# Moving a square root ahead of other copies, sharing a gated add between three engines, and taking the next norm in two halves, in a one-expert layer of a transformer kernel

## What is computed

```python
x = x + _L0_xcond_ref(_layernorm(x), ctx_1024, ...)
x = x + _L0_ffn_ref(_layernorm(x), ...)
x = x + _L1_xcond_ref(_layernorm(x), ctx_1024, ...)
x = x + _L1_ffn_ref(_layernorm(x), Wg, We, be)       # the one-expert layer
x = x + _L2_xcond_ref(ctx_1024, _layernorm(x), ...)  # window attention
x = x + _L2_ffn_ref(...)
...
def _L1_ffn_ref(x, Wg, We, be):                      # h: x as rows of tokens
    probs = softmax(h @ Wg); best = argmax(probs); gate = max(probs)
    mask = one_hot(best) where the token's place in its expert's queue < cap
    out  = (gate * mask) * (h @ We + be)             # all experts share We, be
def _L2_xcond_ref(encoder_outputs, decoder_h_t, src_len, p_t, W_a, W_c):
    score = decoder_h_t @ W_a @ encoder_outputs.T, masked to a window
    context = (softmax(score) * gauss) @ encoder_outputs
    return tanh(concat(context, decoder_h_t) @ W_c.T)
```

## Time and profile before

| | us |
|---|---|
| median of three runs | 1104.2 |
| lowest, highest | 1101.93, 1104.84 |
| the profiled execution's own time | 1099.49 |
| its span, first to last instruction | 1097.7 |

### The profile page before, as it was taken

The page is one execution under the profiler, slowest core; times in us unless marked ns, Lnnn a source line. Parts: engine busy times, 40 slices in busy tenths (PEclk is TensorE's granted clock), DMA queues, the critical chain, the costliest instruction groups (busy, mean ns, idle before and its releaser), DMA issues. The chain is left out here.

```text
span 1097.7 us, 32356 instructions
## 1 busy us (share of the span) xinstructions
PE 938.4 (85%) x12720; PEld 709.1 (65%) x12720; DVE 754.9 (69%) x1651; ACT 596.6 (54%) x1231; POOL 377.3 (34%) x415
## 2 busy tenths in 40 slices
PE   4689998988889998999976689999978999976993
PEld 2457775455666764677754566679835777755992
DVE  4678786646888857888857676657487888761443
ACT  2656565653556654666646675246654676612561
POOL 5033320425333211333200003846723326064442
PEclk8899999989999999999999799999989999967996
DMA  8499980000000000000020001123310112111225
GB/s 248 134 334 322 290 208 3 1 7 5 2 2 3 3 2 1 2 2 3 3 92 1 1 3 57 45 62 91 99 34 17 35 32 68 50 37 54 71 72 170
DMA packets 82013, 73.12 MB, mean 67 GB/s; under 512 B 7600, under 2 KB 77168, under 8 KB 81872
## 3 DMA queue, kind: packets, MB, share of 16 engines
q1 hardware_dynamic: 76656, 61.49, 20.2%
q0 software_dynamic: 4544, 9.36, 2.5%
q10 hardware_dynamic: 672, 0.27, 0.1%
HBM read 24.42 MB, written 46.46 MB: 65 GB/s over the span
## 5 line engine op out<-in xcount | busy, mean ns | idle before, releaser
L1591 ACT ACTIVATE P_t<-ps_pt 128x512 f32<-128x512 f32 x256 | 146.0, 596 | 137.3 <-PE ps_pt L1914 132.3
L1928 PE MATMUL psT<-VB,P_t 128*64 128x18 f32 x4096 | 165.9, 214 | 26.9 <-ACT P_t L1591 19.9
L1928 PEld LDWEIGHTS psT<-VB,P_t 128*64 128x64 f32 x4096 | 140.4, 137 | 66.0 <-ACT P_t L1591 48.6
L956 DVE TENSOR_REDUCE mx<-ps_sc 128x16 f32<-128x1024 f32 x128 | 150.1, 1215 | 16.7 <-PE ps_sc L1902 16.6
L1914 PE MATMUL ps_pt<-cst,work 128*128 128x128 f32 x1024 | 151.5, 281 | 0.0
L967 DVE TENSOR_TENSOR work<-ps_sc,mx 128x1024 f32<-128x1024 f32 x128 | 150.2, 1215 | 0.0
L1554 ACT ACTIVATE work<-work 128x1024 f32<-128x1024 f32 x128 | 128.2, 1048 | 34.3 <-DVE work L967 34.0
L1914 PEld LDWEIGHTS ps_pt<-cst,work 128*128 128x128 f32 x1024 | 112.2, 142 | 5.5 <-ACT work L1554 1.5
L640 POOL TENSOR_TENSOR kbh<-KT,cst 128x512 f32<-128x512 f32 x64 | 65.2, 1039 | 140.2 <-PE ps_sc L1902 107.0
L640 POOL TENSOR_TENSOR rt<-KT,cst 128x512 f32<-128x512 f32 x64 | 65.5, 1044 | 117.5 <-PE ps_sc L1902 117.4
L763 POOL DMA_INDIRECT ys_dram<-work,to_row x78 | 76.4, 979 | 73.0 <-DVE to_row L1446 38.5
(11 more groups left out here) (333 smaller groups left out, 1658.4 us busy)
## 6 DMA issues: line engine op xcount, KB each, us to landing
xs_dram<-slots SPq DMA_DIRECT2D x1, 17160.0 KB, 57.7
xs_dram<-slots SPq DMA_DIRECT2D x1, 17028.0 KB, 123.0
QT<-ys_dram SPq DMA_DIRECT2D x8, 512.0 KB, 6.1
work<-xs_dram SPq DMA_DIRECT2D x39, 65.0 KB, 1.9
work<-xs_dram SPq DMA_DIRECT2D x39, 64.5 KB, 1.9
VB<-L_ffn_W1b_in SPq DMA_DIRECT2D x8, 258.0 KB, 2.6
ctxT<-ctxT_in SPq DMA_DIRECT2D x4, 512.0 KB, 6.9
X<-x_in SPq DMA_DIRECT2D x4, 512.0 KB, 8.0
```

Source lines behind the costliest of these rows:

```text
L956: v.tensor_reduce(mx4[:, :, HPR * t:HPR * t + HPR], sc[:, :, HPR * t:HPR * t + HPR], AX.X, ALU.max).then_inc(max_ready, 1)
L1591: act.activation(P_t[:, 512 * c:512 * c + 512], ps_pt[:, 512 * (c % 2):512 * (c % 2) + 512], ACT.Copy).then_inc(p_evac, 1)
L1928: mm = pe.matmul(psT[64 * b:64 * b + 64, 144 * t + 18 * g:144 * t + 18 * g + 18], P_t[:, at:at + 64], VB[:, UNIT * u + 2 * t + b, g, :, :] ...
```

## The change

- ACT's Sqrt table is loaded explicitly in the last turns of the third attention, and again after the Exp of the logits.
- `rstds` only takes the root; the wait for the finished norm moves into `normalise`, ahead of the first tile. The root of norm 3 stands ahead of `take_a`; two pieces are taken before the normalised tiles, two after the second chunk.
- The four `take_z` ahead of the gates are gone: after the gates ACT gates the four tiles of each even chunk and takes two mixed pieces after each.
- Pool adds the gated even chunks to `X`; DVE adds the odd chunks in one instruction for each tile that multiplies by the gate and adds (`add_gated`).
- Norm 4 is taken in two halves of 16 tiles. The first half's variance comes behind 16 tiles' statistics, the second half's whole chain behind DVE's first normalised half chunk. `NORM_AT` renumbers the counts of the norms for that.
- TensorE waits for all mixed pieces only at step 1 of `attention2`.

```diff
+        NORM_AT = [0, 1, 2, 3, 4, 6, 7]
...
+            def mixture1():
+                pool.wait_ge(x_updated, TILES * 3)
+                for c in range(0, CHUNKS, 2):
+                    xc = X[:, c * TPC:c * TPC + TPC, :]
+                    pool.wait_ge(y_gated, TPC * (c // 2 + 1))
+                    pool.tensor_tensor(xc, Yt[:, c * CHUNK:c * CHUNK + CHUNK].rearrange("p (t d) -> p t d", d=D), xc,
+                                       ALU.add).then_inc(y_added, 1)
+
...
-            def norms_of(ts, i):
+            def norms_of(ln, ts, i):
                 nonlocal n_ln
-                n = n_ln
-                v.wait_ge(stats_ready, TILES * 6 + ts.stop)
+                n, at = n_ln, NORM_AT[ln] + i
+                v.wait_ge(stats_ready, TILES * ln + ts.stop)
                 variance(ts, ln_step, n)
                 n_ln = n + CHAIN_STEPS
                 def finish():
-                    v.wait_ge(rsqrt_ready, 7 + i)
-                    inverse_root(ts, ln_step, n + 5, root_inverted, 7 + i, norm_ready, 2 * (6 + i) + 1)
+                    v.wait_ge(rsqrt_ready, at + 1)
+                    inverse_root(ts, ln_step, n + 5, root_inverted, at + 1, norm_ready, 2 * at + 1)
...
+            def second_norms(ln):
+                norms_of(ln, slice(TILES // 2, TILES), 1)()
+                v.wait_ge(norm_ready, 2 * NORM_AT[ln] + 4)
...
-                def update(k, turn, u, live):
-                    if live(0):
-                        v.wait_ge(y_gated, TPC * (k + 1))
-                        xc = X[:, bass.ds(k * TPC, TPC), :].rearrange("p t d -> p (t d)")
-                        v.tensor_tensor(xc, Yt[:, bass.ds(k * CHUNK, CHUNK)], xc, ALU.add).then_inc(x_updated, TPC)
-                    if live(1):
-                        for t in range(TPC):
-                            tile_stats(4, (k - 1) * TPC + t)
-
-                pipeline(v, CHUNKS, 2, 1, update)
+                def add_gated(t):
+                    ins = v.scalar_tensor_tensor(X[:, t, :], Yt[:, t * D:t * D + D], gate[:, 1, t:t + 1], X[:, t, :], ALU.mult, ALU.add)
+                    if t % TPC == TPC - 1:
+                        ins.then_inc(x_updated, 2 * TPC)
+
+                pairs = CHUNKS // 2
+                for i in range(pairs + 1):
+                    if i < pairs:
+                        for t in range((2 * i + 1) * TPC, (2 * i + 2) * TPC - 1):
+                            add_gated(t)
+                    if i > 0:
+                        for t in range(8 * i - 8, 8 * i):
+                            tile_stats(4, t)
+                    if i == 2:
+                        finish_first = norms_of(4, slice(0, TILES // 2), 0)
+                    if i < pairs:
+                        v.wait_ge(y_added, i + 1)
+                        add_gated((2 * i + 2) * TPC - 1)
+                    if i == pairs - 1:
+                        finish_first()
...
-                norms(4)
...
                         normalise_half(4, k, u)
+                        if isinstance(k, int) and k == 0:
+                            second_norms(4)
...
             def rstds(ln):
-                act.wait_ge(ln_step, 2 + CHAIN_STEPS * ln + 5)
+                act.wait_ge(ln_step, 2 + CHAIN_STEPS * NORM_AT[ln] + 5)
                 act.activation(lnw[:, 4, :], lnw[:, 3, :], ACT.Sqrt).then_inc(rsqrt_ready, 1)
-                act.wait_ge(norm_ready, 2 * ln + 2)
-
-            def root_of(ts, i):
-                act.wait_ge(ln_step, 2 + CHAIN_STEPS * (6 + i) + 5)
+
+            def root_of(ln, ts, i):
+                act.wait_ge(ln_step, 2 + CHAIN_STEPS * (NORM_AT[ln] + i) + 5)
                 act.activation(lnw[:, 4, ts], lnw[:, 3, ts], ACT.Sqrt).then_inc(rsqrt_ready, 1)
             def normalise(ln, k, u):
-                if ln == 6 and isinstance(k, int) and k == 1:
-                    act.wait_ge(norm_ready, 2 * 7 + 2)
+                if isinstance(k, int) and (k == 0 or k == 1 and ln in (4, 6)):
+                    act.wait_ge(norm_ready, 2 * (NORM_AT[ln] + k) + 2)
...
+                    if l == 2 and u == UNITS:
+                        act.preload_act_table_set("sqrt_and_others")
...
             def mixture1():
-                for c in range(4):
+                rstds(3)
+                for c in range(2):
                     take_a(c)
-                rstds(3)
                 def step(k, turn, u, live):
                     normalise(3, k, u)
+                    if isinstance(k, int) and k == 1:
+                        for c in (2, 3):
+                            take_a(c)
                 pipeline(act, CHUNKS, 2, 0, step)
                 for c in (4, 5):
                     take_a(c)
                 act.wait_ge(route_step, 2)
                 act.activation(e_logit, rt[:, 0, :, :], ACT.Exp).then_inc(route_act, 1)
+                act.preload_act_table_set("sqrt_and_others")
                 for c in (6, 7):
                     take_a(c)
-                for c in range(4):
-                    take_z(c)
                 act.wait_ge(keep_step, 5)
                 act.wait_ge(y_kept, 2 * CHUNKS)
-
-                for k in range(CHUNKS):
+                for k in range(0, CHUNKS, 2):
                     for t in range(k * TPC, k * TPC + TPC):
                         row = Yt[:, t * D:t * D + D]
                         act.activation(row, row, ACT.Copy, scale=gate[:, 1, t:t + 1]).then_inc(y_gated, 1)
-                    if k < 4:
-                        take_z(4 + k)
+                    take_z(k)
+                    take_z(k + 1)
+                root_of(4, slice(0, TILES // 2), 0)
...
-                rstds(4)
...
                         normalise(4, k, u)
+                        if isinstance(k, int) and k == 0:
+                            root_of(4, slice(TILES // 2, TILES), 1)
...
-                pe.wait_ge(z_ready, CHUNKS)
                 def step(k, turn, u, live):
                     s, r = u, (u + 1) % 2
+                    if isinstance(k, int) and k == 1:
+                        pe.wait_ge(z_ready, CHUNKS)
```

More of the change, by code:

```diff
@@ L345, in build @@
         y_gated = sem("y_gated")
+        y_added = sem("y_added")
         a_in_psum = sem("a_in_psum")
@@ L746, in _ @@
             pool.memset(maskR[0:2, :], -4.0 * BIG).then_inc(win_filled, 1)
+            def mixture1():
[5 more added lines that the diff above has]
+                                       ALU.add).then_inc(y_added, 1)
+            mixture1()
             def mixture(m):
@@ L859, in norms @@
                 variance(slice(0, TILES), ln_step, n)
-                v.wait_ge(rsqrt_ready, l + 1)
-                inverse_root(slice(0, TILES), ln_step, n + 5, root_inverted, l + 1, norm_ready, 2 * l + 1)
+                at = NORM_AT[l]
+                v.wait_ge(rsqrt_ready, at + 1)
+                inverse_root(slice(0, TILES), ln_step, n + 5, root_inverted, at + 1, norm_ready, 2 * at + 1)
                 n_ln = n + CHAIN_STEPS
+            def second_norms(ln):
+                norms_of(ln, slice(TILES // 2, TILES), 1)()
+                v.wait_ge(norm_ready, 2 * NORM_AT[ln] + 4)
             def variance(ts, counter, n):
@@ L942, in prepare @@
                 v.wait_ge(w_loaded, W_DMAS * 16)
-                v.wait_ge(norm_ready, 2 * ln + 2)
+                v.wait_ge(norm_ready, 2 * NORM_AT[ln] + 2)
                 pipeline(v, CHUNKS, 2, 2, step)
@@ L1112, in rows @@
                                         ALU.mult, ALU.add).then_inc(xn_half, 1)
-                v.wait_ge(norm_ready, 2 * 5 + 2)
+                v.wait_ge(norm_ready, 2 * NORM_AT[5] + 2)
                 rows(0)
@@ L1363, in step @@
                         v.tensor_tensor(p, p, den[s][:, 1, :].unsqueeze(2).broadcast_to([128, TPC, 128]), ALU.mult).then_inc(p2_ready, 1)
-                v.wait_ge(norm_ready, 2 * 4 + 2)
+                v.wait_ge(norm_ready, 2 * NORM_AT[4] + 2)
                 pipeline(v, CHUNKS, 2, 5, step)
@@ L1471, in mixture @@
                         if q == 1:
-                            finish_first = norms_of(slice(0, TILES // 2), 0)
+                            finish_first = norms_of(6, slice(0, TILES // 2), 0)
                         if q == 2:
                             finish_first()
-            def second_norms():
-                norms_of(slice(TILES // 2, TILES), 1)()
-                v.wait_ge(norm_ready, 2 * 7 + 2)
             attention2()
             mixture(0)
-            prepare(3, 6, tau_s, second_norms)
+            prepare(3, 6, tau_s, lambda: second_norms(6))
             attention(3)
@@ L1746, in mixture @@
                     rstds(ln)
+                    act.wait_ge(norm_ready, 2 * NORM_AT[ln] + 2)
                     act.preload_act_table_set("silu_and_others")
@@ L1802, in _ @@
                 if c == 5:
-                    root_of(slice(0, TILES // 2), 0)
-            act.wait_ge(norm_ready, 2 * 6 + 2)
-            prepare(6, lambda: root_of(slice(TILES // 2, TILES), 1))
+                    root_of(6, slice(0, TILES // 2), 0)
```

(1 more changed line is left out.)

## The result

| | before | after |
|---|---|---|
| median, us | 1103.41 (4 runs, 1101.93 to 1104.84) | 1092.76 (4 runs, 1089.06 to 1093.58) |
| the profiled execution's own time | 1099.49 | 1092.79 |
| its span | 1097.7 | 1091.0 |

The account below looks back on a forecast made before the run. It took waits around ACT's blocked roots and gating, at the router norm and from gates to next norm, as the bound; 5.1 + 5.2 + 0.4 = 10.7 us gave 1093.5, forecast 1091.4 to 1096.3, widened 2.7 either side.

Parts of the forecast that it names:

- A: First place, norm before the router: root ahead of context pieces brings the first kept router output 5.1 us earlier.
- B: Second place, gates (G) to the first transposed chunk's copy: G+18.1 instead of 23.27 us, a gain of 5.2.
- C: Third attention: ACT's first key copy no longer waits for the complete norm, a gain of 0.4 us.
- D: TensorE's clock at the second place: same course as before, 3.40, 4.82 and 4.23 us from copy through third maximum.
- The shift passes one for one to the end: Behind the second place's first copy: its earlier time (613.60 before) carries fully to the kernel's end.
- rival 2: Later stages start sooner, then wait for something not moved; gain only 0 to 3 us, 1101 to 1104; chance 0.06.
- The rule against the change: Second place: skill prefers VectorE, GpSimd about twice slower and contending for SBUF; Pool's add doubled, gain 9.7 us.
- Rival 1: Contention and thin covers: Pool's adds double, DVE's tiles take 0.385, first place loses 0.9; gain 6.8, 1097.4; chance 0.10.
- Rival 3: Second place: Pool's add becomes the bound, at 5.1 us each for a 0.3% loss; 1107 to 1110; chance 0.03.
- Rival 4: The change does not do what it says: Sqrt is loaded again before the root; chance left at nothing.

Follow-up runs that it names:

- dve_all: Changed kernel with no gating on ACT and no add on Pool, DVE adding all 32 tiles; ratio to the kernel before 0.9883, gates to first copy 19.50 us.
- one_norm: Changed kernel with norm 4 taken whole again, the rest kept; ratio to the kernel before 0.9918, gates to first copy 18.88 us.
- later_second: Changed kernel with norm 4's second-half chain moved behind the first transposed chunk's copy; ratio to the kernel before 0.9909, gates to first copy 17.82 us.
- a_only: Kernel before with A alone (Sqrt load and norm 3's root ahead of the context pieces); median 1098.36 against 1104.4, ratio 0.9966.
- without_a: Changed kernel with A taken back (four context pieces, then table load and norm 3's root); median 1103.67 against 1104.4, ratio 0.9989.
- stats_beside: Changed kernel with DVE's eight statistics ahead of its adds in each round; ratio to the kernel before 0.9908, gates to first copy 18.58 us.
- combined: Changed kernel with norm 4's second-half chain behind the first copy and Pool's third-attention staging held until the norm completes; ratio to before 0.9898.

## Why the prediction was right

It was 1093.5 us, from a sum of 10.7; the median fell by 10.65, to 1092.76. The single number is better than its working: the sum at the end of the second place was 1.2 too high, the profiled execution then lost 2.8 more, and its own time (1092.79) lies at its kernel's median, where that of before lay 3.9 below its median. So the 1088.8 for the profiled execution was 4.0 too low, and the step of 4.7 up to the median, of which nothing came, made up for it: that the total fits to 0.7 us is luck.

- **A, 5.1 us**: 5.2 measured, in place and alone. Each step came as worked out: root 559.30 (559.2), normalised rows 560.86 (560.7), TensorE at 561.89 (561.9) without a pause and at a clock of 1.00, first kept output 564.52 (564.5). The table load cost nothing: 1.28 from 553.52, in ACT's wait. The new load behind the Exp cost nothing either, with 0.16 us of waiting left for the 0.18 that I had; and the third chunk was turned at 564.51 without a wait, as its thin cover had to allow.
- **B, 5.2 us**: 4.5 measured. The mechanism is right: Pool's first add is out at G+2.7 (2.55), DVE's wait is 1.91 (1.75), the first half's root is hidden. The mis-sized term is DVE's 16 adds: 4.2 predicted, 5.8 measured by the distances of starts (6.1 as busy time, which overlaps). The price of one was about right (0.27 in dve_all, for 0.26), but two groups of four took 2.15 and 1.59 instead of 1.14 beside Pool. Pool's add cost 1.27 for 1.04, also when DVE stood still, within its bounds of 1.04 and 1.45 and covered except the first. Variance, the steps behind the root and the statistics took 0.6 less than their terms, so the statistics ended at G+15.8 (14.6). The rest took 3.0 for 3.5. The cover of Pool's later adds was misread: by the prediction's own terms it is 0.6 to 2.3 us, not 0.9 to 2; they were out 1.6 to 3.6 before DVE asked.
- **What halving is worth.** The prediction said that one chain is hidden and the other left on the path. one_norm shows that the two orders are worth the same (18.88 and 18.79), later_second that the remaining chain was the cost.
- **C, 0.4 us**: a loss of 0.3. This step failed. ACT's keys came earlier, as predicted, but Pool's staging waits for those keys alone, so it started 403.06 and ran into DVE's last two steps of the norm, which took 0.92 and 0.96 instead of 0.19. I had looked only at who waits for the copy next on TensorE. With Pool held back, the gain is 0.45 (3.39 to 2.94), the 0.4 that I had expected.
- **D, the clock as before**: 3.45, 4.82 and 4.24 us for the three chunks, 3.40, 4.82 and 4.23 before. Right for this execution; the other profiles show 11.9 to 14.2 us for the three. That spread goes with the granted clock in the second chunk, most often in code that the edit at hand does not touch: 4.0 to 4.3 us at 0.84 to 0.90 (a_only, without_a, later_second, dve_all), 4.8 at about 0.7 (before, after, one_norm), 5.9 at 0.50 (stats_beside, combined).
- **The shift passes one for one to the end**: 9.5 of it stand at the first row behind the window attention and 6.7 at the end. 1.7 of the difference is the clock in the next router. No wait of rival 2 (something not moved) was found. What remains, 1.1, I can't settle by one execution of each: from that row to the end, the seven variants with the same code there, run where the kernel before took 1104 to 1105 us, needed 437.0 to 444.8 us (the changed kernel 438.7), and the kernel before 436.0.
- **The rule against the change.** DVE's and Pool's rows show that an add with two operands from SBUF slows down beside Pool's add, and that statistics with one operand do not. That is what the Trainium skill, GPSIMD Engine Reference, section Specifications, says of DVE instructions with two SBUF inputs; the trace agrees, with 0.54 and 0.40 us for each add instead of 0.28. By its section Engine selection the add should have stayed on DVE. Its price there, about two times slower, is near what the rows show (1.27 us on Pool; 0.69 for DVE's add of the same 128x512 before the change), but dve_all measures the add on DVE at 0.7 us worse here, so the trace speaks for Pool, by little.
- **Rival 1** had contention at 0.385 for each of the 16 tiles; it was 0.36 on average (5.8 us), so on this term the rival was right and the forecast wrong. Of its doubled Pool add, 1.04 more, 0.2 came (1.27 for 1.04); its loss at the first place did not come. **Rival 3** is far: Pool's adds never passed 1.31 us. **Rival 4** is out: there is no table load before a root.

One thing stays open. By their totals a_only gains 0.34% and without_a 0.11%, less together than the whole change at 1.03%. The distances add up (5.2 and 4.5), the medians' intervals are wide enough to allow it only at their ends, and the profiles show courses 5 us apart in untouched code. In the same rounds as these two, one_norm, whose distances are those of the whole change, gained 0.82%, which narrows the gap but doesn't close it. I take the distances as the measure of the parts.

## What to carry to other kernels

Price a step that is given to GpSimd together with what DVE does beside it: let DVE take one-operand work (statistics, copies) there, and check which waiting Pool work an earlier copy sets free. Cutting a norm in two gains only if nothing that the first chunk needs stands behind the second half's chain. When parts of a change are worth 0.1 to 0.5% and executions differ by as much, measure the distance between two events around the part, not the total.

## What the runs showed of the hardware

- The contention is not in proportion to size. Two DVE steps of two SBUF operands on 128x32 took 0.92 and 0.96 us instead of 0.19 beside Pool instructions of 1.02, as if each waited for one of them; statistics and DVE's copies from PSUM kept their pace beside Pool (1.64 for eight, 1.27 for two).
- TensorE's granted clock falls to its lower level also while TensorE is at work (0.50 at 658.5 to 660.5 in the changed kernel, busy since 654.39), and not in every execution of the same code: its mean over 280 to 300 us was 0.57, 0.60, 0.91 or 1.00. With idle matmuls ahead of a stage the first chunk ran at 1.00 in both kernels that had them; behind it the clock fell in one (0.52) and not in the other.
- One chip ran the same code slower: the kernel before took 1123.54 us there (median of 26 runs), against 1104.4 and 1105.3 on others.
